# A graph network with tiles of the adjacency built on the chip: three small tiles first, tile 0 in one piece behind seven small ones

## The chip, the core and the metric

The kernel runs on one core of a Trainium2 chip. TensorE (PE) multiplies, VectorE (DVE), ScalarE (ACT) and GpSimd (POOL) prepare and finish, SyncE (SP) issues most of the transfers. The metric is device time in microseconds; less is better. Over three runs the kernel before takes 1931.12 us (1929.98 to 1933.58).

## What is computed

A graph network of three layers on 6250 nodes with 256 features and 200,000 edges, then a feed-forward part on the rows that a score picks. Cut to what matters here:

```python
h = jax.nn.relu(_gcn_conv(x, W1, b1, src, dst, norm, num_nodes))
h = jax.nn.relu(_gcn_conv(h, W2, b2, src, dst, norm, num_nodes))
return _gcn_conv(h, W3, b3, src, dst, norm, num_nodes)
# _gcn_conv: h = x @ W; agg = segment_sum(h[src] * norm[:, None], dst); agg + b
# norm = dinv[src] * dinv[dst], dinv = rsqrt(deg), self loops added
# before it: layernorm of x; after it: x + result, layernorm, top-k rows through a gelu FFN
```

The edges are sorted by destination, and low node numbers have many more edges than high ones.

## The kernel before, in words

**Tiles.** The nodes are 49 tiles of 128. The first 32 destination tiles of layer 0 are summed by dense matmuls with a tile of the adjacency (128 destinations by 6272 sources, kept as 49 pieces of 128x128); the other tiles are summed from gathered rows. 34 adjacency tiles are built on the chip, kept in three slots of `space_ring` and stored to `adj` in HBM for the later layers.

**Steps and pairs.** A tile is built from steps. For a step DVE makes two one-hot matrices (`one_hots`, L894 for the low digit and L898 for the high digit, one instruction each for four steps, so for two pairs of steps); PE multiplies them into PSUM (`step`, L1267); ACT copies a finished group into the slot (`evac_group`, L1642). There are 2022 steps, 1011 pairs. Tile 0 has 281 steps, tile 1 135, the following ones 97, 86, 86, then nine tiles of 64, eleven of 43, and nine small ones of 32 (tiles 25 to 33). A step is 147 or 196 columns wide, by tile. The one-hots lie in a ring of 8 pairs: DVE may not write pair j before PE has used pair j-8 (`dve.wait_ge(used, ...)`).

**Units.** A unit is one matmul of 128x512 into the sum of a destination tile: L1300 with a piece of an adjacency tile, L1309 with rows that POOL gathered (L1905). A dense tile has 49 units. When a tile is summed, DVE adds (L938, L940), PE turns the result (L1318) and multiplies it with the next layer's weights (L1326).

**The weave.** The order on PE in layer 0 is written out: pair j, then all units up to `DUE[j]`, a table that the planner fills. DVE runs the same list, five pairs behind: `one_hots(j)`, then `upto(DUE[j - LAG])` with its sums and the like (LAG is 5). Before, `DUE` spreads the units of a tile in proportion over the pairs in which the next tile is built. Since tile 1 is needed while its own diagonal is late, PE adds its self loops (`PE_LOOPS`).

**The preparation.** Ahead of the weave stand the window rows and edges (POOL, L1808 and L1814), the layer norm's moments of x (ACT), the 49 products with the first weights (L1253), the digits of the gathered edges (L819, L821), the counts, the degrees with an overflow chain through POOL (L1892 to L1898) and `dinv`. Tile 0 alone is built in this stage: 140 pairs, `SCAN`. With the factors known, ACT writes the high half and DVE the low half of the scaled features (`high_first` L1627, `low_first` L910), four tiles between two pairs. SP then stores the features to `row_dram` (L2007), which POOL's gathers read, and after that the first adjacency tiles (L2015). Edges that overflow a tile's steps are added to `extra` by a chain of POOL, PE and ACT (`spill`), and a tile's sum reads `extra`.

The rows of the trace name instructions by these lines.

Of the kernel before, what the change touches and what calls it, by code (L numbers as in the profile page):

```python
# [69 lines left out]
TILE_WINDOW = [BASE.index(P * t) for t in range(TD)] + [DWIN]  # L70
# [15 lines left out]
BASE_RUNS = runs_of(0, TD, lambda t: WIDTH_OF[t + 1] == WIDTH_OF[t])  # L86
# [6 lines left out]
         if any(WINDOW_OF.get(s, -1) // P == k for s in range(c * P, c * P + P))]  # L93
TILE_SPANS = [(c, t) for c in range(CHD) for t in range(TD)
              if any(WINDOW_OF[s] in range(TILE_WINDOW[t], TILE_WINDOW[t + 1]) for s in range(c * P, min(c * P + P, DSTEPS)))]
BATCHES = [[0]] + [list(range(c, min(c + 2, CHD))) for c in range(1, CHD, 2)] + [
    list(range(c, min(c + 2, CH))) for c in range(CHD, CH, 2)]
BATCH_AT = [0, 6] + [32 + 4 * b for b in range(len(BATCHES) - 2)]
FIRST_CHUNKS = 3
assert all(k == 0 for c, k in SPANS if c < FIRST_CHUNKS)  # L100


PER_BANK = {4: 2, 3: 3}


def groups_of():
    out = []
    for t in range(TD):
        per = 2 * PER_BANK[WIDTH_OF[t]]
        for w in range(TILE_WINDOW[t], TILE_WINDOW[t + 1], per):  # L110
            out.append((t, w, min(w + per, TILE_WINDOW[t + 1])))
    return out


EGROUPS = groups_of()
# [4 lines left out]
EVACS = len(EGROUPS)  # L120
PER_TILE = EVACS // TD
ASLOTS = 3
# [29 lines left out]
def merged(layer):  # L152
    first = [DENSE[0] - 1] if layer == 1 else []
    dense = [(t, i) for t in first + [t for t in range(DENSE[layer]) if t not in first] for i in range(TILES)]
# [19 lines left out]
SPILL_AT = [END[0] + 38, START[TILES] + 85, START[2 * TILES] + 85]  # L174
OVER_AT = [SPILL_AT[0] + 45, SPILL_AT[1] + 50, SPILL_AT[2] + 50]

# [51 lines left out]
TILE_PAIR = [FIRST[TILE_WINDOW[n]] // 2 for n in range(TD)] + [NPAIR]  # L228
SKEW = 4
LOOP_LAG = 6  # L230
EASE = 24


def units_until(n):
    x = n if n <= EASE or not TWICE else EASE + (n - EASE) * (DENSE[0] - 1 - EASE) / (DENSE[0] - EASE)
    x = min(x, DENSE[0] - 1 + (0.3 if n > DENSE[0] else 0))
    t = int(x)
    whole = END[DENSE_Q[t - 1]] if t else 0
    return whole + int((x - t) * (END[DENSE_Q[t]] - whole))


def due_units():
    due = []
    ends = [units_until(n) for n in range(TD)]
# [11 lines left out]
SCAN = TILE_PAIR[1]  # L256
AHEAD_OF_STEPS, BEFORE = 2, 4
PRODUCT_AT = [t - BEFORE if t < BEFORE else 1 + 2 * (t - BEFORE) for t in range(TILES)]
STATS_BEFORE = 20
EARLY_ROWS = 6  # L260
REST_AT, STEPS_FROM, STEPS_AT = 6, 8, 25
NEXT_AT, WORST_AT, ROUNDS_AT = 28, 31, 34
BOUND_AT = (38, 42, 46, 50)
SPILL_FIRST_AT = 82
DIGITS_AT = max(BATCH_AT[-1] + 6, 70)
GE_AT = [DIGITS_AT + 2 + 2 * r for r in range(W + 1)]
SPARSE_DEG_END = DIGITS_AT + 2 + (TS - TWICE + 1) // 2
COUNTED_AT = max(SPARSE_DEG_END, GE_AT[-1] + 2)
COUNTS_AT = COUNTED_AT + 4
SPOTS_OF_AT = COUNTS_AT + 2  # L270
DEGREES_AT = SPOTS_OF_AT + 12
DINV_AT = DEGREES_AT + 4
assert BATCH_AT[-1] < SPILL_FIRST_AT < DEGREES_AT
LOW_AT = DINV_AT + 3
SETTLED_OF = [max(b + 1 for b, cs in enumerate(BATCHES) if cs[0] < CHD and cs[0] <= min(2 * j + 1, DSTEPS - 1) // P) if j < SCAN else 0
# [3 lines left out]
SLOT_OF = ((DENSE[0] - 1) % 3, 3, DENSE[0] % 3, (DENSE[0] + 1) % 3)  # L279
# [3 lines left out]


PE_LOOPS = 1
# [32 lines left out]
def bank_table():  # L318
    banks, before, last, d = [], [], {}, 0
    for q in sorted(range(len(Q)), key=START.__getitem__):  # L320
        if not IS_DENSE[q]:
            b = 2
        elif q < TILES:
            b = 2 if Q[q] == 2 else (Q[q] + (Q[q] > 2)) % 2
# [12 lines left out]
HOT_FREED_BY, W1_FREED_BY, W2_FREED_BY = FREED_BY[2], FREED_BY[0], FREED_BY[3]  # L337
# [56 lines left out]
LOOPS_AT = [START[DENSE_Q[n]] if n < DENSE[0] else DUE[TILE_PAIR[n + 1] - 1] for n in range(TD)]  # L394
LOOP_PAIR = [min(TILE_PAIR[n + 1] + LOOP_LAG, NPAIR) for n in range(TD)]
LOOP_PAIR[PE_LOOPS] = max(LOOP_PAIR[PE_LOOPS], next(j for j in range(NPAIR) if DUE[j] >= END[DENSE_Q[PE_LOOPS]]) + 6)
assert LOOP_PAIR[PE_LOOPS] < TILE_PAIR[PE_LOOPS + ASLOTS]
LOOPS_OF = by_unit(LOOP_PAIR)
STORES = by_unit([END[PE_LOOPS] + 4 if n == PE_LOOPS else DUE[TILE_PAIR[n + 1] - 1] for n in range(TD)])

THRESHOLDS = len(BASE_RUNS) + 3
# [28 lines left out]
def graph(nc, ctx, space, gathered_in, ones, route, small, smalli, b1_sb, br_b, x, x_turned, dst_rows, dst_over, dst_last, edges, gw, gb, wr, br, w1, b1, w2, b2, pair_dram, out):  # L430
# [25 lines left out]
    ge = area_a[:, 0:(W + 1) * SBASE // 2].bitcast(F16).rearrange("p (r s) -> p r s", r=W + 1)  # L456
    at = (W + 1) * SBASE // 2
    DEG0 = SFIRST[TWICE]
    DEGS = SSTEPS - DEG0
# [233 lines left out]
    with nc.Block() as block:  # L693
        @block.vector
        def _(dve):
# [205 lines left out]
            def add_loops(n):  # L901
                dve.wait_ge(evac, PER_TILE * (n + 1))
                if n == PE_LOOPS:
                    dve.wait_ge(agg_d, n + 1)
# [1219 lines left out]
```

## Time and profile before

| | us |
|---|---|
| median of three runs | 1931.12 |
| the profiled execution | 1930.19 |
| its span | 1928.4 |
| PE busy within the span | 1822.1 |
| DVE busy | 1072.2 |
| POOL busy | 1100.4 |
| ACT busy | 530.6 |

1.8 us of the profiled execution lie outside its span. [...] The preparation takes the first 200 us, the weave of layer 0 goes on to about 808 us, and then follow the other two layers and the feed-forward part. A row of the trace gives start, duration, engine, line, operation, destination and source with the shape, the count, and in brackets the idle time ahead of it with what ended it.

### The profile page before, as it was taken

Reading aid. Unit: us, or ns where it says so; the run is one execution under the profiler, and the core shown is the slowest. Engines: PE = TensorE matmul, PEld = TensorE weight load, DVE = VectorE, ACT = ScalarE, POOL = GpSimd, SP = SyncE. Lnnn points to the kernel's source line nnn. Section 1 sums busy time; section 2 is a strip of 40 time slices with the busy share of each in tenths; the row PEclk is TensorE's granted clock in tenths of the full one; section 3 lists DMA queues with packets and bytes.
Section 4 is the critical chain, followed back from the end, with each engine's and each line's share of the span. In section 5 each row is a group of like instructions: output and inputs, shape, how many; then the busy total and the mean of one; then the engine's idle time right before and its main releaser. Section 6 shows DMA issues by size and latency. Waiting matters only on the chain.

```text
span 1928.4 us, 28276 instructions
## 1 busy us (share of the span) xinstructions
PE 1822.1 (94%) x10122; PEld 1062.6 (55%) x10122; DVE 1072.2 (56%) x2897; ACT 530.6 (28%) x1127; POOL 1100.4 (57%) x1178
## 2 busy tenths in 40 slices
PE   6874989999999999999999999999999999989998
PEld 4753656666565566545555555554444444446755
DVE  7777988788666666542222222223554556876422
ACT  5724234444444455511111111110000000012021
POOL 5401155766666766347777777745777777721401
PEclk9965899999999999999999999999999999999999
DMA  7568245555556566567776777766888988751200
GB/s 270 168 221 281 87 163 187 175 168 191 199 195 208 185 207 213 204 247 245 251 236 232 238 253 237 235 196 245 310 275 296 319 312 284 268 174 72 83 13 23
DMA packets 170448, 403.37 MB, mean 209 GB/s; under 512 B 29419, under 2 KB 122529, under 8 KB 157640
## 3 DMA queue, kind: packets, MB, share of 16 engines
q1 hardware_dynamic: 119720, 263.44, 38.4%
q0 software_dynamic: 50592, 138.13, 22.9%
q8 instruction: 84, 1.38, 0.3%
q14 instruction: 52, 0.43, 0.1%
HBM read 282.57 MB, written 118.89 MB: 208 GB/s over the span
## 4 chain that ended last, share of the span: by engine, by line
PE 83%; DVE 9%; DMA 3%; ACT 2%; issue 2%; POOL 1%; POOLq 0%; DVEq 0%; another core or an unknown queue 0%; ACTq 0%
PE ag L1300 28%; PE pw L1300 20%; PE ag L1309 10%; PE pw L1267 8%; PE pw L1394 3%; PE pw L1326 2%; PE both L1326 2%; PE ag L1407 2%; PE pw L1407 2%; PE ag L1394 1%; PE both L1318 1%; PE ag L1253 1%; ACT space_ring L1642 1%; DVE space_a L910 1%; DVE space_tables L898 1%
## 5 line engine op out<-in xcount | busy, mean ns | idle before, releaser
L1905 POOL DMA_INDIRECT space_rows<-row_dram,src_s x947 | 951.6, 1005 | 372.2 <-issue 200.2
L1300 PE MATMUL ag<-space_a,space_ring 128*128 128x512 f16 x2107 | 621.5, 380 | 3.9 <-DVE space_work L940 3.8
L1267 PE MATMUL pw<-space_tables 128*128 128x147 f16 (+1 forms) x2022 | 324.2, 247 | 51.3 <-DVE space_tables L898 44.9
L1309 PE MATMUL ag<-space_rows,hots 128*128 128x512 f16 x947 | 358.6, 379 | 6.9 <-DVE space_b L940 5.7
L1267 PEld LDWEIGHTS pw<-space_tables 128*128 128x128 f16 x2022 | 220.6, 116 | 227.8 <-DVE space_tables L898 61.5
L1642 ACT ACTIVATE space_ring<-pw 128x784 f16<-128x784 f32 (+1 forms) x257 | 220.4, 858 | 278.2 <-PE pw L1267 272.7
L898 DVE TENSOR_TENSOR space_tables<-iota_two,space_tables 128x588 f16<-128x588 f16 (+1 forms) x506 | 257.6, 509 | 0.0
L1300 PEld LDWEIGHTS ag<-space_a,space_ring 128*128 128x128 f16 x2107 | 198.0, 97 | 102.4 <-DVE space_work L940 4.0
L894 DVE TENSOR_TENSOR space_tables<-iota_many,space_tables 128x512 f16<-128x512 f16 x506 | 212.8, 421 | 27.4 <-PE pw L1267 24.7
L1300 PE MATMUL pw<-space_b,space_ring 128*128 128x512 f16 x735 | 189.3, 379 | 0.0
L1300 PE MATMUL pw<-space_a,space_ring 128*128 128x512 f16 x686 | 167.2, 379 | 0.0
L1652 ACT ACTIVATE space_work<-space_work,per_node 128x256 f32<-128x256 f32 x147 | 73.8, 503 | 324.1 <-DMA space_work<-extra 324.1
L1309 PEld LDWEIGHTS ag<-space_rows,hots 128*128 128x128 f16 x947 | 107.1, 113 | 86.0 <-DVE space_b L940 7.4
L945 DVE SCALAR_TENSOR_TENSOR space_a<-pw,per_node,space_a 128x256 f16<-128x256 f32 x49 | 23.7, 484 | 208.9 <-ACT space_a L1666 208.9
L1660 ACT ACTIVATE space_work<-both,gb_sb 128x128 f32<-128x128 f32 x196 | 61.4, 365 | 226.3 <-PE both L1318 226.2
L1300 PE MATMUL ag<-space_b,space_ring 128*128 128x512 f16 x441 | 115.1, 379 | 0.0
L1300 PEld LDWEIGHTS pw<-space_b,space_ring 128*128 128x128 f16 x735 | 71.8, 98 | 78.4
L1300 PEld LDWEIGHTS pw<-space_a,space_ring 128*128 128x128 f16 x686 | 67.3, 98 | 77.8
L956 DVE TENSOR_TENSOR hots<-iota_many,key_s 128x512 f16<-128x512 f16 x238 | 106.8, 461 | 1.2
L945 DVE SCALAR_TENSOR_TENSOR space_b<-both,per_node,space_b 128x256 f16<-128x256 f32 x49 | 23.7, 484 | 110.9 <-ACT space_b L1666 110.7
L938 DVE SCALAR_TENSOR_TENSOR space_work<-ag,per_node,space_work 128x256 f32<-128x256 f32 x78 | 37.5, 481 | 78.5 <-PE ag L1300 56.2
L1300 PE MATMUL pw<-space_a,space_tables 128*128 128x512 f16 x294 | 76.7, 384 | 0.0
(421 smaller groups left out, 1956.4 us busy)
## 6 DMA issues: line engine op xcount, KB each, us to landing
space_ring<-adj SPq DMA_DIRECT2D x48, 1568.0 KB, 7.7
adj<-space_ring SPq DMA_DIRECT2D x34, 1568.0 KB, 6.1
space_tables<-adj SPq DMA_DIRECT2D x17, 1568.0 KB, 7.4
extra<-hots SPq DMA_DIRECT2D x3, 6272.0 KB, 22.4
space_work<-extra SPq DMA_DIRECT2D x147, 128.0 KB
space_rows<-row_dram,src_s POOLq DMA_INDIRECT x947, 4.0
space_b<-in_x_turned SPq DMA_DIRECT2D x7, 896.0 KB, 14.2
space_a<-in_x SPq DMA_DIRECT2D x7, 896.0 KB, 5.9
```

The costliest lines, as they stand in the source:

```text
L894: dve.tensor_tensor(olo[:, r], iota_many[:], slo[:, 2 * j:2 * j + 4].unsqueeze(1).broadcast_to([P, P, 4]), ALU.is_equal)
L898: dve.tensor_tensor(ohi[:, r, :, 0:n], iota_two[:, 0:n].unsqueeze(1).broadcast_to([P, 2, n, 2]), keys.unsqueeze(2).broadcast_to([P, 2, n, ...
L956: dve.tensor_tensor(hots_area[:, n % (HOTS // 4)], iota_many[:], key_s[:, s:s + 4].unsqueeze(1).broadcast_to([P, P, 4]), ALU.is_equal).the ...
L1267: pe.matmul(pw[v % 2][:, half, at_c:at_c + n], olo[:, j % RING // 2, :, j % 2 * 2 + i], ohi[:, j % RING // 2, j % 2, 0:n, i], start=s == F ...
L1300: mm = pe.matmul(bank(q), a[:, k, :], hh[l][:, k, :], start=i == 0 and not own, stop=i == TILES - 1)
L1309: pe.matmul(bank(q), hots_area[:, hot_at, :, g - SPOT_GROUPS[SPOT_GROUP_OF[g]][0]], slots[g % GR], start=i == 1, stop=i == n).then_inc(g_u ...
L1326: mm = pe.matmul(ph[l - 1], fresh[:, q % 2, f, :], gw_sb[:, l, f, :], start=f == 0, stop=f == HALVES - 1)
L1394: mm = pe.matmul(bank_of(hidden_banks[h % 3])[:, 0:n], w1_sb[:, k, m * P:(m + 1) * P], xt[c][:, k, 0:n], start=k == 0, stop=k == HALVES - 1)
L1407: mm = pe.matmul(bank_of(out_banks[s % 2])[0:n, 0:D], hid[c % 2][:, m, i * P:i * P + n], w2_sb[:, m, :], start=m == 0, stop=m == HM - 1)
L1642: act.activation(target[:, :, d:d + n].rearrange("p s (h d) -> p s h d", h=2), pw[v % 2][:, :, 0:n // 2 * TILES].rearrange("p h (d s) -> p ...
L1652: act.activation(ep[:, q % 2], ep[:, q % 2], ACT.Copy, scale=unfactor[:, l, t:t + 1]).then_inc(e_scaled, 1)
L1905: pool.indirect_dma_start(slots[g % GR], None, row_dram[STEP_LAYER[g]], bass.IndirectOffsetOnAxis(src_s[:, s:s + 1], 0)).then_inc(g_in[g % ...
```

## The change

The order of building, the preparation and the planner's table are new.

- Tiles are built in the order 29, 30, 31, 25, 26, 27, 28, 0, 1, 2, ..., 24, 32, 33 (`BUILD`). The preparation holds 52 pairs: tiles 29, 30 and 31 and four pairs of tile 25.
- After the 52nd pair PE runs the 98 units of tiles 29 and 30, alternating between the two, as the scaled features arrive; `low_first` stands alone on DVE, 49 in a row, and `high_first` on ACT.
- `DUE` is now a line through the whole weave by cost, capped at the last unit of a tile that has been built (`most`). The cap holds from pair 209 on to about pair 875: at 384 units for pairs 209 to 255, then each time up to the end of the tile that has just been finished, 441 at pair 256, 505 at 323, 565 at 372, and so on.
- Three of the seven groups of x get their moments on ACT, four on DVE. All ten window rows are fetched ahead of the edges, edges of six chunks instead of three come first, products stand after every pair, and the digits have another layout.
- SP stores the first three adjacency tiles ahead of the features. The third waits for its self loops, which DVE adds at pair 54. Two of the three big areas of zeros, and the pair area, are cleared in pieces later.
- The first sum's overflow (`spill(0)`) is at unit 130 instead of 87, and `extra` is read from unit 132 on.

```diff
+FIRST_BUILT = (29, 30, 31)
+LAST_BUILT = 24
+BUILD = [(t, g) for t in FIRST_BUILT + (25, 26) for g in range(GROUPS_OF_TILE)]
+BUILD += [(t, g) for t in (27, 28, 0) for g in range(GROUPS_OF_TILE)]
+BUILD += [(t, g) for t in list(range(1, LAST_BUILT + 1)) + [32, 33] for g in range(GROUPS_OF_TILE)]
...
+FIRST_CHUNKS = 6
...
+        dense = [(t, i) for i in range(TILES) for t in tiles[0:2]] + [(t, i) for t in tiles[2:] for i in range(TILES)]
...
-SPILL_AT = [END[0] + 38, START[TILES] + 85, START[2 * TILES] + 85]
+SPILL_AT = [2 * TILES + 32, START[TILES] + 85, START[2 * TILES] + 85]
...
+SCAN = 52
...
-    for j in range(NPAIR):
-        total = 0
-        for n in range(1, TD):
-            a, b = TILE_PAIR[n] + SKEW, TILE_PAIR[n + 1] + SKEW
-            done = min(max(j + 1 - a, 0), b - a) / (b - a)
-            total += int(done * (ends[n] - ends[n - 1]))
-        due.append(total)
+    due = [0] * SCAN
+    for j in range(SCAN, NPAIR):
+        want = first + int((last - first) * (cost[j] - cost[SCAN]) / (cost[NPAIR - 1] - cost[SCAN]))
+        most = max([e for e, p in zip(ends, END_PAIR) if p + SKEW <= j + 1])
...
+        due.append(max(due[-1], least, min(most, want)))
...
-SCAN = TILE_PAIR[1]
...
+ACT_GROUPS, DVE_GROUPS = (0, 2, 4), (1, 3, 5, 6)
...
-LOOP_PAIR = [min(TILE_PAIR[n + 1] + LOOP_LAG, NPAIR) for n in range(TD)]
+LOOP_PAIR = [min(p + LOOP_LAG, NPAIR) for p in END_PAIR]
...
                 pair(j)
             j = SCAN
+            units(2 * TILES)
             while j < NPAIR:
...
+            for n in range(len(FIRST_BUILT)):
+                store_tile(n)
             for g in range(GROUPS):
                 sp.wait_ge(lo_1, g * KC + KC)
```

PE in the middle of the weave, before: a tile of 64 steps. L1267 are steps, two to a pair; L1300 and L1309 are dense and gathered units, L1318 turns a finished sum.

```order
L1267 MATMUL pw<-space_tables 128x196 x2
L1300 MATMUL ag<-space_a,space_ring 128x512 x2
L1267 MATMUL pw<-space_tables 128x196 x2
L1300 MATMUL ag<-space_a,space_ring 128x512 x2
L1318 MATMUL both<-ident,space_work 128x128 x2
L1267 MATMUL pw<-space_tables 128x196 x2
L1300 MATMUL ag<-space_a,space_ring 128x512
```

Each pair stands between one or two units. PE around the end of such a tile, after (L1334 are steps, L1362 and L1371 dense and gathered units).

```order
L1362 MATMUL ag<-space_a,space_ring 128x512 x3
L1371 MATMUL ag<-space_rows,hots 128x512
L1362 MATMUL ag<-space_a,space_ring 128x512 x2
L1334 MATMUL pw<-space_tables 128x196 x64
L1362 MATMUL ag<-space_a,space_ring 128x512
L1371 MATMUL ag<-space_rows,hots 128x512
L1362 MATMUL ag<-space_a,space_ring 128x512 x3
```

All 64 steps (32 pairs) stand in one row with no unit among them, and the 57 to 65 units of a tile's turn stand together on either side.

DVE at the scaled features, before (L910 is `low_first`, L894 and L898 the one-hots of two pairs).

```order
L910 SCALAR_TENSOR_TENSOR space_a<-space_b,per_node,space_a 128x256 x4
L894 TENSOR_TENSOR space_tables<-iota_many,space_tables 128x512
L898 TENSOR_TENSOR space_tables<-iota_two,space_tables 128x2x294
L910 SCALAR_TENSOR_TENSOR space_a<-space_b,per_node,space_a 128x256 x4
L894 TENSOR_TENSOR space_tables<-iota_many,space_tables 128x512
```

And after (L983 is `low_first`, L968 and L972 the one-hots, L979 adds the self loops of the third tile).

```order
L983 SCALAR_TENSOR_TENSOR space_a<-space_b,per_node,space_a 128x256 x49
L968 TENSOR_TENSOR space_tables<-iota_many,space_tables 128x512
L972 TENSOR_TENSOR space_tables<-iota_two,space_tables 128x784
L979 TENSOR_TENSOR space_ring<-space_ring,ident 128x128
L968 TENSOR_TENSOR space_tables<-iota_many,space_tables 128x512
```

The pairs between the groups are gone, and the 49 instructions stand in one row.

SP at the end of the preparation, before (L1994 clears `extra`, L2003 the pair area, L2000 reads the degrees, L2007 stores the features, L2015 adjacency tiles).

```order
L1994 DMA extra<-hots 128x49x256 x2
L2000 DMA by_tile<-deg_dram 49x128
L1994 DMA extra<-hots 128x49x256
L2003 DMA pair_dram<-hots 1792x1x256
L2003 DMA pair_dram<-hots 1024x1x256
L2007 DMA row_dram<-space_a 128x7x512 x7
L2015 DMA adj<-space_ring 128x6272 x3
```

And after (L2051, L2054, L2059, L2065 in the same roles; L2100 reads `extra` for a sum).

```order
L2051 DMA extra<-space_tables 128x49x256
L2054 DMA by_tile<-deg_dram 49x128
L2059 DMA adj<-space_ring 128x6272 x3
L2065 DMA row_dram<-space_a 128x7x512 x7
L2059 DMA adj<-space_ring 128x6272
L2100 DMA space_work<-extra 128x256 x3
```

The three tiles of the adjacency have moved ahead of the features, and the clears behind the weave's beginning.

## Rows read from the trace of the kernel before

**Rows 1.** The page: busy time by engine, and the chain that ended last.
```profile
PE 1822.1 (94%) x10122; PEld 1062.6 (55%) x10122; DVE 1072.2 (56%) x2897; ACT 530.6 (28%) x1127; POOL 1100.4 (57%) x1178
...
PE 83%; DVE 9%; DMA 3%; ACT 2%; issue 2%; POOL 1%; POOLq 0%; DVEq 0%; another core or an unknown queue 0%; ACTq 0%
```

**Rows 2.** Windows: length, busy time of PE (count), granted clock, DMA share, GB/s.
```profile
42.00:48.00 6.00, 4.42 (x30) 1.00 0.01 3
...
186.00:192.00 6.00, 1.37 (x8) 0.50 1.04 342
...
300.00:400.00 100.00, 100.00 (x655) 1.00 0.54 180
```

**Rows 3.** Windows of DVE: length, busy time (count), clock, DMA share, GB/s.
```profile
300.00:400.00 100.00, 82.48 (x203) 1.00 0.54 180
```

**Rows 4.** Timeline of PE: pairs of 147 and 196 columns between units.
```profile
206.03 0.30 PE L1267 MATMUL pw<-space_tables 128*128 128x147 f16 x2
206.16 0.38 PE L1300 MATMUL ag<-space_a,space_ring 128*128 128x512 f16 x1
206.38 0.30 PE L1267 MATMUL pw<-space_tables 128*128 128x147 f16 x2
...
231.20 0.38 PE L1300 MATMUL ag<-space_a,space_ring 128*128 128x512 f16 x1
231.41 0.34 PE L1267 MATMUL pw<-space_tables 128*128 128x196 f16 x2
231.59 0.38 PE L1300 MATMUL ag<-space_a,space_ring 128*128 128x512 f16 x1
```

**Rows 5.** Timeline of DVE: one-hots for two pairs, both widths.
```profile
206.49 0.41 DVE L894 TENSOR_TENSOR space_tables<-iota_many,space_tables 128x512 f16<-128x512 f16 x1
206.83 0.45 DVE L898 TENSOR_TENSOR space_tables<-iota_two,space_tables 128x588 f16<-128x588 f16 x1
207.20 0.41 DVE L894 TENSOR_TENSOR space_tables<-iota_many,space_tables 128x512 f16<-128x512 f16 x1
...
226.99 0.42 DVE L894 TENSOR_TENSOR space_tables<-iota_many,space_tables 128x512 f16<-128x512 f16 x1
227.32 0.56 DVE L898 TENSOR_TENSOR space_tables<-iota_two,space_tables 128x784 f16<-128x784 f16 x1
227.80 0.42 DVE L894 TENSOR_TENSOR space_tables<-iota_many,space_tables 128x512 f16<-128x512 f16 x1
```

**Rows 6.** Timeline of PE: pairs alone, then the first units of the weave.
```profile
196.53 2.69 PE L1267 MATMUL pw<-space_tables 128*128 128x147 f16 x16 [0.42 <-DVE space_tables L898]
...
201.32 0.63 PE L1300 MATMUL ag<-space_a,space_ring 128*128 128x512 f16 x1
```

**Rows 7.** Windows of all engines around the weave's start and one stall.
```profile
195.80:201.20 5.40, 4.42 (x30) 2.79 (x29) 5.40 (x17) 1.06 (x2) 0.05 (x1) 0.50 0.79 263
201.30:204.70 3.40, 3.40 (x18) 2.01 (x17) 3.40 (x11) 0.00 (x0) 3.40 (x1) 0.50 0.97 406
...
266.10:273.00 6.90, 5.47 (x23) 3.06 (x24) 5.17 (x14) 1.30 (x2) 5.21 (x6) 0.51 0.91 333
```

**Rows 8.** Timelines of the preparation: PE's first pair, POOL's fetches, DVE's start of `low_first`.
```profile
38.04 0.43 PE L1267 MATMUL pw<-space_tables 128*128 128x147 f16 x2 [1.44 <-DVE space_tables L898]
...
25.32 0.95 POOL L1808 DMA_INDIRECT space_rows<-in_dst_rows,tile_i  x1 [0.31 <-issue]
26.57 0.95 POOL L1808 DMA_INDIRECT space_rows<-in_dst_rows,tile_i  x1 [0.30 <-issue]
...
163.95 1.66 DVE L910 SCALAR_TENSOR_TENSOR space_a<-space_b,per_node,space_a 128x256 f16<-128x256 f32 x4
```

**Rows 9.** SP's and POOL's timelines: the features stored, and POOL's wait for them.
```profile
173.99 22.17 SPq L2007 DMA_DIRECT2D row_dram<-space_a  x7
...
201.15 4.81 POOL L1879 DMA_INDIRECT space_rows<-row_dram,space_rows  x1 [33.97 <-DMA row_dram<-space_a]
...
208.59 0.87 POOL L1885 TENSOR_SCALAR space_rows<-iota,space_rows 128x128 f16<-128x128 f16 x1 [0.21 <-POOL space_rows L1884]
```

**Rows 10.** The page: DMA issues, KB each and us to landing.
```profile
adj<-space_ring SPq DMA_DIRECT2D x34, 1568.0 KB, 6.1
```

**Rows 11.** Timelines of PE and POOL: the overflow chain of the first sum.
```profile
240.94 0.38 PE L1341 MATMUL both<-space_rows 128*128 128x512 f16 x1
...
257.03 5.10 POOL L1897 TENSOR_SCALAR space_rows<-space_rows 128x1 f32<-128x1 f32 x1 [8.68 <-DMA extra<-space_rows]
...
267.53 0.61 PE L1300 MATMUL ag<-space_a,space_ring 128*128 128x512 f16 x1 [3.84 <-DVE space_work L940]
...
151.35 0.24 POOL L1897 TENSOR_SCALAR space_rows<-space_rows 128x1 f32<-128x1 f32 x1 [6.94 <-DMA deg_dram<-space_rows]
```

More of the change, by code:

```diff
@@ L152, in merged @@
 def merged(layer):
-    first = [DENSE[0] - 1] if layer == 1 else []
-    dense = [(t, i) for t in first + [t for t in range(DENSE[layer]) if t not in first] for i in range(TILES)]
+    if layer == 0:
+        tiles = [t for t in BUILT if t < DENSE[0]]
+        dense = [(t, i) for i in range(TILES) for t in tiles[0:2]] + [(t, i) for t in tiles[2:] for i in range(TILES)]
+    else:
+        first = [LAST_BUILT] if layer == 1 else []
+        dense = [(t, i) for t in first + [t for t in range(DENSE[layer]) if t not in first] for i in range(TILES)]
     sparse = []
@@ L252, in due_units @@
     return due
 DUE = due_units()
-SCAN = TILE_PAIR[1]
[L257 to L266, printed above, removed]
+BEFORE = 4
+PRODUCT_AT = [t - BEFORE if t < BEFORE else t - BEFORE + 1 for t in range(TILES)]
@@ L753, in lows @@
                 done(dve.scalar_tensor_tensor(step_cols[:, ks, 2], first_col[:, ks], float(-P), low[:, ks], ALU.mult, ALU.add),
-                     f"low of step zero {ks.start}")
+                     "low of step zero")
             def place_steps(i):
@@ L829, in hot_tiles @@
                     c, t = TILE_SPANS[i]
-                    noted(dve.tensor_scalar(tile_base[:, i:i + 1], step_base[:, c, 0:1], float(W - 1 - P * t), None, ALU.add))
-                dve.wait_ge(c_dve, steps["all"])
-                for i in range(first, last_one):
-                    noted(dve.tensor_scalar(tile_hot[:, i], iota16[:, 0:P + 4], tile_base[:, i:i + 1], None, ALU.is_equal),
-                          f"hot tile {i}")
+                    noted(dve.tensor_scalar(tile_hot[:, i], iota16[:, 0:P + 4], float(P * t - W + 1), step_base[:, c, 0:1],
+                                            ALU.add, ALU.is_equal), f"hot tile {i}")
             def step_masks():
@@ L1296, in unit @@
                             pe.wait_ge(lo_s, (l - 1) * TILES + i + 1)
-                    own = l == 0 and t == PE_LOOPS
-                    if own and i == 0:
-                        pe.matmul(bank(q), ident16[:], hh[l][:, t, :], start=True, stop=False)
-                    mm = pe.matmul(bank(q), a[:, k, :], hh[l][:, k, :], start=i == 0 and not own, stop=i == TILES - 1)
+                    mm = pe.matmul(bank(q), a[:, k, :], hh[l][:, k, :], start=i == 0, stop=i == TILES - 1)
                     if i == TILES - 1:
@@ L1482, in chunk_steps @@
                     mm.then_inc(p_steps, 1)
-            pe.wait_ge(c_dve, steps["low of step zero 0"])
-            for c in range(FIRST_CHUNKS):
+            pe.wait_ge(c_dve, steps["low of step zero"])
+            for c in range(CH):
                 chunk_steps(c)
-            for t in range(AHEAD_OF_STEPS, BEFORE):
-                product_first(t)
             def colsums(name):
@@ L1711, in _ @@
             done_stats = 0
-            for t in range(AHEAD_OF_STEPS):
-                stat_op(done_stats)
-                done_stats += 1
-                out_first(t)
             while done_stats < STATS_BEFORE:
@@ L1718, in _ @@
                 done_stats += 1
-            for t in range(AHEAD_OF_STEPS, BEFORE):
-                out_first(t)
+                if done_stats % 4 == 0:
+                    out_first(done_stats // 4 - 1)
             settle(0)
```

421 lines of the change are left out of this document (245 added, 176 removed).

## The prediction

> **What bounds the kernel now.** I read the page first, then windows of the weave, then the timelines of PE and DVE inside it. PE is busy for 94% of the span and carries 83% of the chain that ended last [rows 1], so a change must either take work off PE or fill or open gaps on it. From 300 to 400 us PE is busy for the whole window at full clock [rows 2], DVE for 82.48 of the same 100 us [rows 3]. So in layer 0 PE is the bound, and DVE has little to spare. That holds only because units stand among the pairs, and the two timelines show why. A unit takes PE 0.214 us (206.16 to 206.38, 231.20 to 231.41). A pair of 147 columns takes it 0.137 (206.03 to 206.16, 206.38 to about 206.52), one of 196 columns 0.18 (231.41 to 231.59) [rows 4]. DVE makes the one-hots of two pairs in 0.71 us (206.49 to 207.20) and 0.81 us (226.99 to 227.80) [rows 5], that is 0.356 and 0.406 us for one pair. A pair alone therefore costs DVE more than twice what it costs PE. With one unit behind it the two engines are about even, with two PE is the later. The row of 16 steps ahead of the first unit shows the other pace: eight pairs in 2.69 us, 0.34 each, at the half clock [rows 6].
>
> **The change part by part.** I work against the profiled execution, 1930.2 us, 0.9 us under the median of the runs.
>
> *The beginning.* Before, the first unit starts at 201.32 [rows 6], behind all 140 pairs of tile 0, and `low_first` begins at 163.95 [rows 8]. After, `low_first` stands behind only 52 pairs. The order shows two pairs between its groups of four, some 24 pairs in all, so DVE is spared 140-24-52 = 64 pairs ahead of it, 64 x 0.356 = 23 us. Against that, four more window rows and three more chunks of edges come ahead of the first pair, 7 fetches 1.25 us apart (25.32 to 26.57), so the first pair moves from 38.04 to about 47 or, with its own wait, 50 [rows 8]; that is 9 to 12 us. And DVE takes 28 tiles of statistics, which no row shows; I bound one by 0.25 and 0.6 us (its other operations on 256 columns lie near 0.4, as in the four of L910 in 1.66 us [rows 8]), 7 to 17 us, and take 12. The sum is near zero, so I keep 163.95 for the start, with 145 and 180 as ends, since PE's many small matmuls on the degrees and POOL's overflow chain also stand in it. `low_first` alone needs 49 x 0.40 = 20 us. PE's 98 units need 98 x 0.214 = 21 us and follow it; they begin at half clock, which before lasted for 3.4 us of units (201.30 to 204.70 [rows 7]) and costs half of that, 1.7. So PE is through them at about 187. There it has done 98 units that it had not before at 201.3, and 88 pairs fewer; pairs done weigh 140 x 0.137 = 19.2 before and 52 x 0.18 = 9.4 after. **Gain: 14.3 + 21 - 9.8 = 25 us**, between 9 and 45.
>
> *The wait for the first sum.* This is a new one. SP holds seven stores of features, and ahead of them now the third adjacency tile, whose self loops DVE adds at pair 54, behind the 98 units, so at about 188. Everything queued on SP waits with it. That tile takes 6.1 us [rows 10], and the features took SP 22.17 us [rows 9] beside clears that are now elsewhere; the DMA engines moved 342 GB/s then [rows 2], by which 6.4 MB are 18.7. So the features are out at 188 + 6 + 19 = 213, before at 201.15. From there POOL needs 201.15 to 209.46 = 8.3 us until its one-hot is ready [rows 9]. Before, that was long done when PE came to the overflow matmul at 240.94; from this matmul to the first sum's release of PE at 267.53 it took 26.6 us, of which POOL spent 5.10 on an operation that took 0.24 elsewhere [rows 11]. With a standing DVE I bound the chain by 20 and 26.6. The sum is then done at 213 + 8.3 + 23 = 244 (242 to 248). PE stands at the overflow matmul at unit 130, and again at unit 147, whose bank waits for this sum. From 187 it has 49 units and 27 pairs, 49 x 0.214 + 27 x 0.18 = 15.4 us, so it would be there at 202. **Loss: 42 us**, bounds 30 to 50; before it was 3.84 us at the same place [rows 11] and about 3.4 more for the 6.9 us at half clock that followed [rows 7]. So +42 + 3.4 after, - 7 before: **+38 us**.
>
> *The bursts.* The cap in the new table leaves stretches without a unit, as the order on PE shows: 47, 67, 49, 43, 43, nine times 32, and seven times 21 or 22 pairs. Before there are none of such length. While PE runs 57 to 65 units in a row (some 13 us) DVE can go on, but only to pair J+6: it builds five pairs and then stands in the sums of that burst, and the ring of eight would stop it two later. So of k pairs six are ready, and the others come at DVE's pace while PE waits for each. The loss of one stretch is (k-6) times 0.22 (0.356 - 0.137) or 0.226 (0.406 - 0.18) us. Narrow ones: 41 + 61 + 37 + 37 pairs and 7 x 15.5 = 108, together 284 x 0.219 = 62 us. Wide ones: 43 + 9 x 26 = 277, x 0.226 = 63 us. **Loss: 125 us.** Its cover would have to be units among these pairs, and those are all spent. Bounds: 105 if DVE gets eight pairs ahead and not six (20 stretches x 2 x 0.22 = 9) and some pairs beside PE's standing run quicker; 145 if each burst also begins and ends with 1 us of signals.
>
> *At nothing.* The clears in pieces, the slots and the later layers' order change transfers that PE doesn't wait for: in 300 to 400 us the DMA share is 0.54 [rows 2]. With the cover gone they could cost a few us. The units and steps are as many as before.
>
> **Sum:** 1930 - 25 + 38 + 125 = 2068, and 2 for signals: **2070 us**.
>
> **The rivals.** *The clock falls in the stretches.* With pairs alone PE works for 0.137 of 0.356 us. From 186 to 192 us, with 8 matmuls in 6 us, the clock is at its lower level; from 42 to 48, with 30 matmuls, at the upper [rows 2]; from 195.8 to 201.2, with 30 in 5.4 us, it was low and stayed low [rows 7]. So the rows leave it open. If it falls, each burst begins at half clock for about 3.4 us [rows 7] and loses 1.7, and the six ready pairs and the change-over may double that: 20 bursts x 1.7 to 3.4 = 34 to 68 us, so 2104 to 2138, I take **2115**. [...]
>
> *The preparation becomes much shorter.* If PE and POOL are not in the way and DVE is freed early, `low_first` could start near 125. Every part behind it moves along, and the loss for the first sum stays, since its chain starts from the same point: 2070 - 39 = **2031**; from 2050 down I count it to this case. Against it stand DVE's added statistics and the 49 products that PE still has ahead of it.
>
> *The stretches are covered, and the kernel is faster.* Its place is the one-hots: if DVE, with PE not beside it, made pairs at PE's pace, the 125 us would vanish and 2070 - 125 = 1945 be left. It decides the sign from the point where `low_first` also begins by 145, 19 earlier, which is the early end of its bounds: 1926 there, **1915** at 134. Against it stand the equal durations of L894 and L898 in rows where DVE never waits [rows 5], and the row of pairs alone, at 0.34 [rows 6].
>
> *The change doesn't do what it says*, that is, its stretches exist in the table but the cap never bites because PE is late anyway: then only the beginning and the first sum count, 1930 - 25 + 38 = 1943, and with the bounds of these two, 1915 to 1970.
>
> **How the numbers follow.** The forecast, 2050 to 2095, gets 0.47; the falling clock, above 2095, 0.2; the short preparation, 1975 to 2050, 0.19; the last two together, 1900 to 1975, 0.14, of which 0.07 lie below 1926, 0.03 within 0.2% of the kernel before (3.9 us, about what a measurement of this kernel can tell from no change), and 0.04 above. The range leaves out these 0.14 and the last 0.06 of the falling clock: 1975 to 2130. Slower by over 0.2% has 0.9, the same 0.03, faster 0.07.
>
> **What would show it.** In the profile after: stretches of steps on PE between about 300 and 900 us with a wait for L972, DVE's one-hots, ahead of nearly each, some 125 us of idle time in all, in a page that shows PE busy well under 94%; one wait of about 40 us on PE near 200 to 245 us, split over the overflow matmul and the first unit of a third bank use; features leaving SP at about 195; first unit near 165. The granted clock in the stretches decides the first rival. Wrong would I be if PE showed idle time of under 60 us in the weave, or if DVE's one-hots took under 0.3 us a pair there.

## The result, and the profile after

| kernel | median us | runs | against before |
|---|---|---|---|
| before | 1931.36 | 4 | |
| after | 2112.68 | 4 (2111.65 to 2116.80) | 1.0942 (1.0923 to 1.0961) |

The change costs 181.3 us. The time lies in the stated range of 1975 to 2130 and 43 us above the forecast of 2070, at the number that the falling clock was given (2115). Both mechanisms, DVE's pace in the bursts and the falling clock, turned out to be at work, and with other shares than either sum had: the time lies above the forecast's own band of 2050 to 2095, in the one that was given to the falling clock, but most of the excess came from the stretches.

The page of the kernel after: busy time by engine, the granted clock in 40 slices in tenths, the chain that ended last by engine.

```profile
span 2109.9 us, 28166 instructions
...
PE 1920.3 (91%) x10113; PEld 1073.8 (51%) x10113; DVE 1074.6 (51%) x2909; ACT 502.7 (24%) x1011; POOL 1077.1 (51%) x1186
...
PEclk8888896979999989899999999999999999999999
...
PE 75%; DVE 17%; DMA 4%; ACT 2%; issue 1%; POOL 1%; POOLq 0%; DVEq 0%; another core or an unknown queue 0%; ACTq 0%
```

Against [rows 1], DVE's share of the chain has gone from 9 to 17% while its busy time is the same to 3 us: it does no more work, but PE waits for it. PE is busy longer although it does the same work, which is a sign of the lower clock. In the profiles of this case the granted clock has two values, 1.00, called the upper level here, and 0.50, the lower; a window over both shows their mean, 0.91 in the one from 268 to 988 us below. A unit of the kernel before lasts 0.63 us at 201.32 [rows 6], where the clock is 0.50 [rows 7], and 0.38 at 206.16 [rows 4], where it is 1.00 (205.50 to 207.00), and counts as busy for as long.

Where the time went is seen best from the place at which layer 0 ends. Windows of PE, after and then before (length, busy time and count, granted clock, DMA share, GB/s):

```profile
268.00:988.00 720.00, 632.76 (x3625) 0.91 0.46 152
...
988.00:2110.00 1122.00, 1091.28 (x5042) 0.99 0.64 219
```

```profile
267.50:808.00 540.50, 536.19 (x3397) 0.99 0.57 192
808.00:1929.00 1121.00, 1088.99 (x5030) 0.99 0.64 219
```

Layer 0 ends at about 988 us and no longer at 808. What follows takes 1122 and 1121 us. So all of the loss lies ahead of that point, and nearly all of it in the weave. There PE's idle time and its releasers are these (PE, 188 to 988 us after, by line; busy us and mean ns, idle time ahead):

```profile
L1362 PE MATMUL ag<-space_a,space_ring 128*128 128x512 f16 x1447 | 423.7, 396 | 12.5 <-DVE space_ring L979 8.1 <-DVE space_work L1013 4.3
L1334 PE MATMUL pw<-space_tables 128*128 128x147 f16 (+1 forms) x1910 | 270.8, 262 | 82.0 <-DVE space_tables L972 59.1 <-ACT space_ring L1707 20.6 <-issue 0.2
L1371 PE MATMUL ag<-space_rows,hots 128*128 128x512 f16 x325 | 127.9, 394 | 0.0
```

The steps (L1334) wait for DVE's one-hots (L972) for 59.1 us, for ACT's copies (L1707) for 20.6, and the first unit of a burst waits for the self loops (L979) for 8.1. Before, 201 to 808 us, the steps waited 6.3 us in all.

One wide stretch shows how it goes. PE's timeline of the kernel after, the end of a burst and the stretch behind it:

```profile
488.27 0.38 PE L1362 MATMUL ag<-space_a,space_ring 128*128 128x512 f16 x1
488.49 1.05 PE L1334 MATMUL pw<-space_tables 128*128 128x196 f16 x10
490.56 0.54 PE L1334 MATMUL pw<-space_tables 128*128 128x196 f16 x4 [1.02 <-DVE space_tables L972]
491.38 0.55 PE L1334 MATMUL pw<-space_tables 128*128 128x196 f16 x4 [0.27 <-DVE space_tables L972]
492.19 0.55 PE L1334 MATMUL pw<-space_tables 128*128 128x196 f16 x4 [0.27 <-DVE space_tables L972]
...
502.17 0.59 PE L1362 MATMUL ag<-space_a,space_ring 128*128 128x512 f16 x2 [0.67 <-DVE space_ring L979]
```

Five pairs (10 steps) are ready and run at once; then PE waits for 1.02 us, and from there it gets two pairs every 0.81 us (490.56, 491.38, 492.19), which is DVE's pace of [rows 5] to the hundredth. The first wait is longer because DVE comes out of the burst with sums to do. DVE's timeline at the same place:

```profile
488.69 0.48 DVE L1011 SCALAR_TENSOR_TENSOR space_work<-ag,per_node,space_work 128x256 f32<-128x256 f32 x1 [7.09 <-PE ag L1362]
489.21 0.48 DVE L1013 SCALAR_TENSOR_TENSOR space_work<-ag,per_node,space_work 128x256 f32<-128x256 f32 x1
489.61 0.41 DVE L968 TENSOR_TENSOR space_tables<-iota_many,space_tables 128x512 f16<-128x512 f16 x1
```

It stood for 7.09 us until the burst's last units were done, made two sums, and only at 489.61 began the next one-hots. At the end of the stretch the wait for the self loops (0.67 us) comes on top. So the 32 pairs last from 488.49 to 502.17, 13.7 us; among units they would take PE 32 x 0.18 = 5.8. The loss is 7.9 us, where (k-6) counts 5.9.

Summed in this way over PE's timeline, the 22 stretches of 17 to 67 pairs lose 160 us. The (k-6) count gives 127 for the same 22.

A narrow stretch looks different, though it has the same cause. Again PE's timeline of the kernel after:

```profile
460.56 7.74 PE L1334 MATMUL pw<-space_tables 128*128 128x147 f16 x44 [0.25 <-DVE space_tables L972]
468.47 0.28 PE L1334 MATMUL pw<-space_tables 128*128 128x98 f16 x1 [0.17 <-DVE space_tables L972]
469.22 1.66 PE L1334 MATMUL pw<-space_tables 128*128 128x196 f16 x9 [0.47 <-ACT space_ring L1707]
471.13 1.87 PE L1362 MATMUL ag<-space_a,space_ring 128*128 128x512 f16 x4 [0.25 <-DVE space_ring L979]
```

44 steps, 22 pairs, in 7.74 us: 0.35 us a pair, DVE's pace again. But the row shows hardly any waiting, because PE has dropped to the lower clock (0.50 from 460.56 to 468.30) and its longer matmuls fill the time. So the waits in the table understate what DVE's pace costs: 82.0 us of idle time ahead of steps stand against a loss of 160. The burst behind it begins with 4 units in 1.87 us, also at the lower clock (0.50 from 471.13 to 473.00).

### The profile page after: what moved, and what is told of

It is laid out like the page before. It is cut to its first block, busy times and chain, and to the rows that moved or that the text cites. A ratio compares the mean times of both kernels' runs of the same rounds, so it can differ in the third digit from the quotient of the medians.

```text
span 2109.9 us, 28166 instructions
## 1 busy us (share of the span) xinstructions
PE 1920.3 (91%) x10113; PEld 1073.8 (51%) x10113; DVE 1074.6 (51%) x2909; ACT 502.7 (24%) x1011; POOL 1077.1 (51%) x1186
## 4 chain that ended last, share of the span: by engine, by line
PE 75%; DVE 17%; DMA 4%; ACT 2%; issue 1%; POOL 1%; POOLq 0%; DVEq 0%; another core or an unknown queue 0%; ACTq 0%
PE ag L1362 27%; PE pw L1362 19%; PE ag L1371 9%; DVE space_tables L972 5%; DVE space_tables L968 4%; PE pw L1334 4%; PE pw L1456 3%; PE both L1388 2%; PE pw L1388 2%; DMA space_rows<-extra,space_rows 2%; PE ag L1469 2%; PE pw L1469 2%; PE ag L1456 1%; ACT space_ring L1707 1%; PE both L1380 1%
## 5 line engine op out<-in xcount | busy, mean ns | idle before, releaser
L1961 POOL DMA_INDIRECT space_rows<-row_dram,src_s x947 | 941.1, 994 | 596.5 <-PE ag L1371 396.9
L1362 PE MATMUL ag<-space_a,space_ring 128*128 128x512 f16 x2107 | 586.6, 392 | 15.1 <-DVE space_ring L979 8.1
L1334 PE MATMUL pw<-space_tables 128*128 128x147 f16 (+1 forms) x2022 | 291.7, 263 | 90.8 <-DVE space_tables L972 67.5
L1371 PE MATMUL ag<-space_rows,hots 128*128 128x512 f16 x947 | 363.8, 384 | 6.1 <-DVE space_b L1013 5.8
L1362 PEld LDWEIGHTS ag<-space_a,space_ring 128*128 128x128 f16 x2107 | 207.7, 100 | 218.3 <-issue 36.6
L1334 PEld LDWEIGHTS pw<-space_tables 128*128 128x128 f16 x2022 | 188.7, 120 | 222.8 <-DVE space_tables L972 120.6
L1707 ACT ACTIVATE space_ring<-pw 128x784 f16<-128x784 f32 (+1 forms) x257 | 218.2, 858 | 277.3 <-PE pw L1334 263.5
L972 DVE TENSOR_TENSOR space_tables<-iota_two,space_tables 128x588 f16<-128x588 f16 (+1 forms) x506 | 259.4, 513 | 0.0
L968 DVE TENSOR_TENSOR space_tables<-iota_many,space_tables 128x512 f16<-128x512 f16 x506 | 214.1, 423 | 31.0 <-PE pw L1334 28.7
L1362 PE MATMUL pw<-space_b,space_ring 128*128 128x512 f16 x735 | 189.3, 379 | 0.0
L1362 PE MATMUL pw<-space_a,space_ring 128*128 128x512 f16 x686 | 167.2, 379 | 0.0
L1371 PEld LDWEIGHTS ag<-space_rows,hots 128*128 128x128 f16 x947 | 107.7, 114 | 107.8 <-DVE space_b L1013 7.5
L1362 PE MATMUL ag<-space_b,space_ring 128*128 128x512 f16 x441 | 115.1, 379 | 0.0
L1362 PEld LDWEIGHTS pw<-space_b,space_ring 128*128 128x128 f16 x735 | 71.9, 98 | 78.5
L1362 PEld LDWEIGHTS pw<-space_a,space_ring 128*128 128x128 f16 x686 | 67.3, 99 | 77.8
L1362 PE MATMUL pw<-space_a,space_tables 128*128 128x512 f16 x294 | 78.1, 389 | 0.0
```

Of the source, the lines that this page charges most:

```text
L968: dve.tensor_tensor(olo[:, r], iota_many[:], slo[:, 2 * j:2 * j + 4].unsqueeze(1).broadcast_to([P, P, 4]), ALU.is_equal)
L972: dve.tensor_tensor(ohi[:, r, :, 0:n], iota_two[:, 0:n].unsqueeze(1).broadcast_to([P, 2, n, 2]), keys.unsqueeze(2).broadcast_to([P, 2, n, ...
L1334: pe.matmul(pw[v % 2][:, half, at_c:at_c + n], olo[:, j % RING // 2, :, j % 2 * 2 + i], ohi[:, j % RING // 2, j % 2, 0:n, i], start=s == F ...
L1362: mm = pe.matmul(bank(q), a[:, k, :], hh[l][:, k, :], start=i == 0, stop=i == TILES - 1)
L1371: pe.matmul(bank(q), hots_area[:, hot_at, :, g - SPOT_GROUPS[SPOT_GROUP_OF[g]][0]], slots[g % GR], start=i == 1, stop=i == n).then_inc(g_u ...
L1707: act.activation(target[:, :, d:d + n].rearrange("p s (h d) -> p s h d", h=2), pw[v % 2][:, :, 0:n // 2 * TILES].rearrange("p h (d s) -> p ...
```

## The experiments

### The planner's line alone

Only `want` is bent: as in the changed kernel up to pair 112, and from there along straight pieces that spend one tile's units while the next is built.

```diff
+    whole = END_PAIR[len(FIRST_BUILT) + 3]
+    knots = [(whole, first + int((last - first) * (cost[whole] - cost[SCAN]) / (cost[NPAIR - 1] - cost[SCAN])))]
+    knots += [(END_PAIR[n] + SKEW - 1, ends[n - 1]) for n in range(len(FIRST_BUILT) + 4, len(ends))] + [(NPAIR - 1, last)]
...
+        if j > knots[0][0]:
+            a, b = max(k for k in knots if k[0] < j), min(k for k in knots if k[0] >= j)
+            want = a[1] + int((b[1] - a[1]) * (j - a[0]) / (b[0] - a[0]))
```

> The changed kernel with its planner's line bent: up to pair 112 as it is, from there straight pieces that use up the units of one tile while the next is built, so no stretch of pairs without a unit is longer than four. All else is the changed kernel. If the stretches make the loss (PE idle for about 87 us between 268 and 988 us, and half clock in part of it), the 181 us go except for the other two terms, a gain of about 19 us in the beginning and a wait of 18 us for the first sum with some microseconds at half clock: 1920 to 1960 us, with the granted clock back at 0.96 or more. Rival: the loss lies in the new order of tiles, the slots and their transfers, and not in where the units stand: 2050 us or more.

Measured: 1945.27 us (1940.90 to 1949.22), a ratio of 1.0057 (1.0035 to 1.0079). Of the 181 us, 167 are gone with this line. PE in its weave, 188 to 830 us:

```profile
L1368 PE MATMUL ag<-space_a,space_ring 128*128 128x512 f16 x1503 | 473.1, 381 | 4.5 <-DVE space_work L1019 4.5
L1340 PE MATMUL pw<-space_tables 128*128 128x147 f16 (+1 forms) x1918 | 305.3, 241 | 14.2 <-ACT space_ring L1713 8.4 <-DVE space_tables L978 5.0
```

The wait for one-hots falls from 59.1 to 5.0 us, that for copies from 20.6 to 8.4, the one for self loops is gone, and a unit's mean is 381 ns again and not 396. The order of tiles, the slots and the transfers are those of the changed kernel, so by themselves they don't make the loss.

### The same bursts in the kernel before

The mirror: the kernel before, with a tile's units let go at once when it is built.

```diff
-            done = min(max(j + 1 - a, 0), b - a) / (b - a)
+            done = float(j + 1 > a)
```

> The kernel before with one line changed: a tile's units are let go at once when the tile is built, instead of in proportion over the next tile's pairs. Order of tiles, preparation and transfers stay. By the term of the bursts: narrow stretches 62 + 37 + 37 + 11 x 15.5 = 306 pairs beyond six, wide ones 42 + 9 x 26 + 8 x 10 = 356, so 67 + 80 = 147 us, and with the clock and copies seen in the changed kernel up to 190: 2080 to 2125. Rival: the bursts only hurt together with the new order of tiles: under 2000.

Measured: 2119.70 us (2118.63 to 2121.55), 187 us more than the kernel before. The old order of tiles with bursts is as slow as the new one. PE there, 201 to 1000 us:

```profile
L1267 PE MATMUL pw<-space_tables 128*128 128x196 f16 (+1 forms) x1747 | 243.6, 273 | 90.2 <-DVE space_tables L898 54.5 <-ACT space_ring L1642 33.1
```

It is the same picture with the same two waits. Taken away from the new order the bursts end the loss, put into the old one they make it, so it belongs to them.

### Shorter bursts, three times as many

From pair 256 on a tile's units go in three parts.

```diff
-        most = max([e for e, p in zip(ends, END_PAIR) if p + SKEW <= j + 1])
+        n = sum(p + SKEW <= j + 1 for p in END_PAIR[:len(ends)])
+        most = ends[n - 1]
+        if j >= END_PAIR[len(FIRST_BUILT) + 4] + SKEW - 1 and n < len(ends):
+            part = 1 + 3 * (j + 1 - END_PAIR[n - 1] - SKEW) // (END_PAIR[n] - END_PAIR[n - 1])
+            most = ends[n - 2] + (most - ends[n - 2]) * part // 3
```

> The changed kernel with the units of a tile let go in three parts over the next tile's pairs, from pair 256 on, in place of one. Stretches become a third as long and three times as many. If each stretch of k pairs costs (k-6) times 0.22 or 0.226 us, the narrow ones fall from 243 such pairs to 131 and the wide ones from 277 to 157: 24.5 + 27 = 52 us less than 2112.7, so 2050 to 2065. Rival: a burst has a fixed price (signals, ACT's copy, the clock at its start), so three times as many bursts cost more or give nothing back: 2105 or more.

Measured: 2054.51 us (2047.46 to 2057.60), 58 us less than the kernel after, where (k-6) gave 52. So most of the price goes with the pairs that are not ready, and not with the number of bursts. The agreement with 52 is closer than the parts: summed over the timeline as above, the stretches lose 106 us and no longer 160, that is 54 less; the clock fell less too (0.97 from 268 to 930 us, after 0.91 from 268 to 988), which helped; and the preparation ended 8 us later in this profile, which hurt. PE's wait for ACT's copies goes the other way, 30.5 us here against 20.6. PE, 188 to 940 us:

```profile
L1338 PE MATMUL pw<-space_tables 128*128 128x147 f16 (+1 forms) x1918 | 239.2, 247 | 63.5 <-DVE space_tables L976 31.0 <-ACT space_ring L1711 30.5
```

### DVE two pairs further ahead

```diff
-LAG = 5
+LAG = 7
```

> The changed kernel with one number changed: DVE runs its list of sums seven pairs behind and not five, so it may have two more pairs of one-hots ready when a burst ends, as far as the ring of eight allows. By the term of the bursts each of 20 stretches gets 1 to 2 pairs shorter, 0.22 us each: 4 to 9 us less, 2104 to 2109. Rival: the pairs behind a burst wait for ACT's copy and not for DVE: within 2 us of 2112.7.

Measured: 2103.79 us (2097.11 to 2105.07), 8.9 less, at the far end of what was expected. PE's timeline at the stretch shown above, in the fastest of the four runs:

```profile
487.29 1.40 PE L1334 MATMUL pw<-space_tables 128*128 128x196 f16 x14
489.36 0.55 PE L1334 MATMUL pw<-space_tables 128*128 128x196 f16 x4 [0.67 <-DVE space_tables L972]
```

Seven pairs (14 steps) are ready here and five with the lag of 5: what is ready behind a burst is the lag, at most a pair more, and the ring of eight is not what limits it. The first wait is shorter as well, 0.67 us instead of 1.02.

### Something for PE to do in the stretches

From the seventh pair of a stretch on, each step is followed by a matmul with the same weights and a moving operand of zeros, added to the same sum.

```diff
+FILL = [j for j in range(209, NPAIR) if j >= 7 and DUE[j] == DUE[j - 7]]
...
+                if j in FILL:
+                    mm = pe.matmul(pw[v % 2][:, half, at_c:at_c + n], olo[:, j % RING // 2, :, j % 2 * 2 + i], zeros.bitcast(F16)[:, 0:n],
+                                   start=False, stop=end, skip_group_check=True)
```

> The changed kernel with one more matmul behind each step in the stretches, from the seventh pair without a unit on (550 pairs): the same weights, a moving operand of zeros, added to the same sum. DVE's pace stays; PE has twice the matmuls there (0.27 of 0.36 us and 0.36 of 0.41 us a pair at full clock). If the clock falls because PE does too little in the stretches, it now stays up between 268 and 920 us, bursts begin at full clock, and 25 to 60 us come back: 2055 to 2090. Rival: the clock falls for another reason, such as the stop at a burst's end: no change or up to 20 us more.

Measured: 2092.93 us (2091.44 to 2098.28), 20 us less for 1100 matmuls more. That is just under the 25 that was the least expected. The clock did what the expectation's first theory says. Windows of PE with the filler, and of the kernel after:

```profile
268.00:500.00 232.00, 221.74 (x1755) 1.00 0.44 146
500.00:720.00 220.00, 208.37 (x1451) 1.00 0.47 156
720.00:900.00 180.00, 166.57 (x1121) 1.00 0.48 160
```

```profile
268.00:500.00 232.00, 207.89 (x1241) 0.85 0.42 137
500.00:720.00 220.00, 184.45 (x1038) 0.98 0.49 164
720.00:900.00 180.00, 159.73 (x846) 0.88 0.44 147
```

So it is what PE has to do in the stretches that decides the clock here: with the 1100 matmuls more it is 1.00 in all three windows, where it was 0.85, 0.98 and 0.88, and 20 us come back. It fell mainly in the narrow stretches (268 to 500 and 720 to 900); from 500 to 720, where the stretches are wide, it stayed up almost always (0.98). That is why it cost 20 us and not the 34 to 68 that the rival multiplied out over 20 bursts. Where the 20 us lie, PE's timelines tell. The 22 stretches lose 161 us with the filler and 160 without, so in them the lower clock costs nothing, since DVE sets the pace either way, and the filler costs nothing there either. Behind them, in the bursts, PE ran at the lower level for about 45 us in all in the kernel after and not at all with the filler (1.00 from 268 to 960 us). Half of that time, 23 us, is what it lost there, as an estimate from a unit's 0.415 us at the lower level (four from 471.13 to 472.79 in the kernel after, clock 0.50) and 0.214 at the upper (206.16 to 206.38 in [rows 4]).

### The features ahead of the third tile

SP stores the features before the third adjacency tile, once in the changed kernel and once with the planner's line bent.

```diff
-            for n in range(len(FIRST_BUILT)):
+            for n in range(len(FIRST_BUILT) - 1):
                 store_tile(n)
             for g in range(GROUPS):
...
+            store_tile(len(FIRST_BUILT) - 1)
```

> As woven, and SP stores the features ahead of the third adjacency tile instead of behind it, so that they leave as they are made. In the changed kernel SP stood at that third tile from 163.4 to 188.9 us. If the wait for the first sum hangs on the features, the overflow matmul comes 12 to 18 us earlier and the time falls by as much against woven (10 to 20 us). Rival: the wait hangs on POOL's chain or on the DMA engines themselves: within 3 us of woven.

> The changed kernel, stretches and all, with the features stored ahead of the third adjacency tile. If the wait for the first sum adds to the stretches one for one, as the prediction sums them, 12 to 17 us less, as between woven and woven_rows: 2096 to 2101. Rival: the time won there is given back in the stretches, where DVE sets the pace: within 4 us of 2112.7.

Measured: 1930.31 us with the bent line (1927.58 to 1933.61), 15.0 less than without the reordering, and a ratio to the kernel before of 0.9984 (0.9974 to 0.9994); 2100.42 us in the changed kernel (2098.60 to 2104.60), 12.3 less. The wait adds to the stretches nearly one for one. The medians of such runs come from spans that differ by 5 to 8 us between executions, so 15.0 and 12.3 are not two sizes. SP's timeline, the changed kernel first, then the one with the features ahead:

```profile
163.38 25.47 SPq L2059 DMA_DIRECT2D adj<-space_ring  x3
188.90 15.99 SPq L2065 DMA_DIRECT2D row_dram<-space_a  x7
```

```profile
167.79 0.81 SPq L2059 DMA_DIRECT2D adj<-space_ring  x2
175.88 17.03 SPq L2065 DMA_DIRECT2D row_dram<-space_a  x7
```

SP stands in the third tile's wait until 188.9 and only then issues the features; reordered, it starts at 175.88 and issues each group as `low_first` finishes it. PE's wait at the overflow matmul, 14.06 us, vanishes; the later one at the first sum's bank stays, 6.16 us here and 4.33 in the kernel after:

```profile
220.64 0.61 PE L1362 MATMUL ag<-space_a,space_ring 128*128 128x512 f16 x1 [6.16 <-DVE space_work L1013]
```

### Both remedies and the longer lag

> woven_rows with DVE's list of sums seven pairs behind. Without long stretches DVE is not what PE waits for (5.0 us of waits on the one-hots are left, 8.4 on ACT's copy), so 0 to 4 us less than woven_rows: 1925 to 1931. Rival: sums that come later hold PE up at a bank: 1935 or more.

Measured over 8 runs: 1925.17 us (1921.87 to 1931.54), a ratio of 0.9963 (0.9949 to 0.9977). This beats both kernels, by 0.37% against the one before. Whether it is the lag by itself was asked of the kernel before:

> The kernel before with DVE's list of sums seven pairs behind instead of five, nothing else. PE there waits for the one-hots of the weave for only 0.5 us and for ACT's copy 5.2, so no change: within 3 us of the kernel before. Rival: the later list is worth the same 5 us in any order of tiles (woven_rows against woven_rows_lag7: 1930.3 and 1925.2): 1925 to 1928.

Measured: 1932.04 us over 11 runs, a ratio of 1.0000 (0.9991 to 1.0009). So the lag alone is worth nothing there. The small gain needs the new order of work, by itself (0.16% in `woven_rows`) or together with the lag. PE's wait for one-hots in the weave fell from 5.0 us (`woven_rows`) to 2.0. The two medians lie 5.1 us apart; the rest of that is not explained, and the two were not timed side by side.

## Why the prediction was right, step by step

**What bounds the kernel** held: a pair without a unit goes at DVE's pace, 0.81 us for two wide pairs before and after.

**The bursts** were the largest term and had the right mechanism, but were sized too small: 125 forecast, 160 lost in the stretches by the timeline, and 167 taken away by `woven`, the clock's share included. DVE's pace was right, and so was the change with the number of pairs (54 in `thirds`, where the count says 52). What the count had wrong lies around DVE's pace. At the beginning five pairs are ready and not six, and the wait behind them is 1.0 us long, as DVE makes its sums first. Later in a stretch PE waits for ACT's copies (20.6 us in all) and at its end for the self loops (8.1), for which the forecast had 2 us "for signals". Of the signs that were named, the 125 us of idle time came as 82.0 ahead of steps; the rest hides in matmuls that take longer at the lower clock (a unit's mean is 396 ns and a step's 262, in `woven` 381 and 241).

**The clock** was put into a rival and should have been in the sum. The rows of before left it open, as the text said. What settles it is the kernel after beside the run with the filler: a mean clock of 0.85 and 0.88 in the windows with narrow stretches and of 0.98 from 500 to 720 us, where they are wide, and 1.00 in all three with the filler. The rival's size was overrated, 34 to 68 us for the 20 that the filler brought back.

**The wait for the first sum** came where it was placed, at units 130 and 147, and was oversized: 14.06 and 4.33 us of idle time, and some 10 us at the lower clock behind them (a mean of 0.79 from 220 to 240 us is 8.4 at the lower level, and 2.4 lie ahead of that) that cost half by the estimate from a unit's 0.415 and 0.214 us, so about 23.5 us instead of 42 + 3.4. The way to it was right: POOL got the features at 212.91, forecast 213. The failed step is the bound of 20 to 26.6 us for the overflow chain. PE and POOL of the kernel after:

```profile
217.56 0.59 PE L1403 MATMUL both<-space_rows 128*128 128x512 f16 x1 [14.06 <-POOLq L1898]
...
229.52 0.61 PE L1362 MATMUL ag<-space_a,space_ring 128*128 128x512 f16 x1 [4.33 <-DVE space_work L1013]
...
212.91 0.94 POOL L1935 DMA_INDIRECT space_rows<-row_dram,space_rows  x1 [33.64 <-DMA row_dram<-space_a]
219.25 0.72 POOL L1948 TENSOR_TENSOR space_rows<-space_rows 128x256 f32<-128x256 f32 x1 [3.07 <-DMA space_rows<-extra,space_rows]
224.77 0.23 POOL L1953 TENSOR_SCALAR space_rows<-space_rows 128x1 f32<-128x1 f32 x1 [1.79 <-DMA extra<-space_rows]
```

From the overflow matmul to the release it took 12.0 us, before 26.6 [rows 11]. POOL's steps that took 4.81 [rows 9] and 5.10 us [rows 11] while DVE was at work (busy for 4.81 and 5.02 of them) took 0.94 and 0.23 here, where DVE stood, and a transfer waited for 8.68 us came in 1.79. The prediction had taken this off one operation and not off all of them.

**The beginning** was a little too good. DVE's `low_first` began at 168.04, forecast 163.95, and PE was through the 98 units at 192.4, forecast 187:

```profile
168.04 19.52 DVE L983 SCALAR_TENSOR_TENSOR space_a<-space_b,per_node,space_a 128x256 f16<-128x256 f32 x49 [0.68 <-ACT space_a L1689]
...
168.67 23.73 PE L1362 MATMUL ag<-space_a,space_ring 128*128 128x512 f16 x98 [2.67 <-DVE space_a L983]
```

So 20 us were gained instead of 25. In the profile of `woven_rows` `low_first` begins only at 177.38, and the gain there is about 10.

**The sum.** Without its 2 us for signals the forecast was 2068. It was low by 35 in the stretches and by 20 in the clock, high by some 22 at the first sum, and low by 5 in the beginning: 2068 + 35 + 20 - 22 + 5 = 2106. About 7 us to 2113 are left over. Waits that no term held and that the bent line does not take away are of that size (14.2 us on one-hots and copies in `woven`, 6.3 before), but no run shows that they are the remainder. That `woven` took away 167 and not 180 goes in part with its preparation, which ended 8 us later in its profile than in that of the kernel after. So the sign and the mechanisms were right on their merits; that the number is off by 43 and not by 65 is luck, since the first sum was oversized while the bursts and the clock were undersized.

**The rivals.** The short preparation did not come. The stretches were not covered. The table did what it says. The falling clock came, in part.

## What to carry to other kernels

Where two engines alternate in a written order, the balance has to hold in every stretch as long as the lead that one has over the other, not over the whole: here the same units and pairs cost 167 us more when they stood apart, with a lead of five pairs in a ring of eight. A schedule that runs work "as soon as it is ready" uses up the cover that the slower producer needs later. And a queue that issues in order should not hold a wait for something late ahead of what others wait for: one store moved behind seven was worth 12 to 15 us.

## What the runs showed of the hardware that was not expected

In this kernel a slow partner hid behind a fallen clock. In one narrow stretch of the kernel after the pairs come at DVE's pace at either level: two in 0.71 us from 457.72 to 458.43 at a clock of 1.00, 22 in 7.74 us from 460.56 to 468.30 at 0.50. But at the lower one PE's steps last longer (a mean of 322 ns from 461 to 468 us, 236 from 457.0 to 460.4) and it shows as busy: the row at 460.56 covers 7.74 us without a wait inside it. The preparation ran at either level of the clock in the same code: from 120 to 145 us the granted clock was 0.93 in the profile of the kernel after and 0.54 in that of `woven_rows`, whose instructions up to there are the same, and `low_first` began 9 us later in the latter. The rows, in that order (length, busy time and count of PE, its weight loads, DVE, ACT and POOL, then clock, DMA share, GB/s):

```profile
120.00:145.00 25.00, 22.41 (x423) 18.02 (x423) 9.05 (x22) 7.26 (x15) 0.00 (x0) 0.93 0.40 132
```

```profile
120.00:145.00 25.00, 22.12 (x305) 16.70 (x305) 9.22 (x18) 4.75 (x10) 0.00 (x0) 0.54 0.47 155
```

With PE busy for about the same time, it got through 423 matmuls in the one and 305 in the other. The other profiles with this beginning lie between: 0.87 twice, 0.84, 0.78, 0.66 and 0.64. What decides it, no run tested. The comparisons between runs above carry a share of this spread, which is up to 9 us between these profiles.

And POOL's small operations took a fifth or less of their time where DVE stood still (0.94 for 4.81, 0.23 for 5.10 us). The other profiles show the same for the first of them, POOL's fetch of the features for the overflow. It took 0.94 us in all eight profiles in which DVE stood meanwhile, and 4.81, 3.24 and 42.92 us in the three in which DVE was at work. The longest is that of `before_lag7` (POOL's timeline, then a window with the columns as above):

```profile
202.04 42.92 POOL L1879 DMA_INDIRECT space_rows<-row_dram,space_rows  x1 [33.93 <-DMA row_dram<-space_a]
```

```profile
202.00:244.90 42.90, 39.14 (x300) 25.48 (x298) 42.13 (x112) 11.45 (x14) 42.86 (x1) 0.96 0.09 38
```

DVE is busy for 42.13 of these 42.90 us, with instructions that follow each other without a gap, and the fetch ends 0.8 us after the last of them. Not every operation of POOL beside a busy DVE was long: in `woven_rows` an addition took 0.74 us (at 214.30), the one that took 2.91 in the kernel before (at 242.42), with DVE busy throughout both. Whether instructions of DVE hold POOL up, and which, no run tested.
